# Cross-attention, feed-forward and quantised layers in one kernel: values with keys on the partitions, weights converted into the token buffers, first loads in order of use, fewer warm-up products

## What is computed

```python
query = layernorm(x) @ w_q.T        # 2 x 512 tokens, 1024 features
key   = ctx_4096 @ w_k.T            # 2 x 1024 context rows, 256 features
value = ctx_4096 @ w_v.T            # 2 x 1024 context rows, 256 features
...
att = softmax(query_h @ key_g.T / sqrt(32), masked) @ value_g
x = x + att @ w_out.T
```

## Time and profile before

| | us |
|---|---|
| median of 3 runs | 1073.83 (1072.63 to 1076.23) |
| the profiled execution | 1075.11 |
| its span in the trace | 1073.3 |
| PE busy | 1032.0 |
| DVE busy | 874.6 |
| stage a, start to the last product of PE | 200.5 |

### The profile page before, as it was taken

The page is one execution under the profiler, slowest core; times in us unless marked ns, Lnnn a source line. Parts: engine busy times, 40 slices in busy tenths (PEclk is TensorE's granted clock), DMA queues, the critical chain, the costliest instruction groups (busy, mean ns, idle before and its releaser), DMA issues. The chain is left out here.

```text
span 1073.3 us, 20195 instructions
## 1 busy us (share of the span) xinstructions
PE 1032.0 (96%) x7174; PEld 780.3 (73%) x7174; DVE 874.6 (81%) x1881; ACT 663.5 (62%) x1127; POOL 93.8 (9%) x85
## 2 busy tenths in 40 slices
PE   8999999999999999999999999999999999956978
PEld 7888888777777777777777777776888887534637
DVE  5764544799999999999999999975764895879998
ACT  5332320498989899898998989862331114635826
POOL 0221011200000000000000000000002112400000
PEclk9999999999999999999999999999999999987989
DMA  8548779841123232123323212158315000000003
GB/s 328 182 166 297 258 262 280 314 121 37 45 75 73 68 73 70 37 45 73 73 68 73 66 39 48 50 202 276 118 59 171 0 0 1 1 1 1 1 1 156
DMA packets 55568, 112.95 MB, mean 105 GB/s; under 512 B 7724, under 2 KB 21164, under 8 KB 55388
## 3 DMA queue, kind: packets, MB, share of 16 engines
q1 hardware_dynamic: 55452, 112.26, 33.6%
q0 software_dynamic: 64, 0.00, 0.0%
HBM read 83.99 MB, written 27.26 MB: 104 GB/s over the span
## 5 line engine op out<-in xcount | busy, mean ns | idle before, releaser
L898 DVE CUSTOM_DVE_ANT_0 XS<-b_psS,b_mbias 128x1024 f32<-128x1024 f32 x256 | 311.1, 1215 | 0.9 <-PE b_psS L778 0.7
L853 ACT ACTIVATE XS<-XS,b_mins 128x1024 f32<-128x1024 f32 x256 | 295.5, 1154 | 10.1 <-DVE b_mins L898 9.5
L811 PEld LDWEIGHTS b_psT<-ident,XS 128*128 128x128 f32 x2048 | 229.9, 140 | 65.8 <-issue 47.6
L811 PE MATMUL b_psT<-ident,XS 128*128 128x128 f32 x2048 | 271.9, 276 | 1.6 <-ACT b_PT L861 1.6
L907 DVE COPY b_PT<-b_psT 128x512 f32<-128x512 f32 x256 | 176.9, 691 | 26.8 <-PE b_psT L811 25.1
L861 ACT COPY b_PT<-b_psT 128x512 f32<-128x512 f32 x256 | 149.7, 585 | 38.8 <-PE b_psT L811 30.8
L778 PE MATMUL b_psS<-XTh 128*128 128x512 f32 x512 | 155.9, 422 | 0.7 <-PEq L115 0.6
L792 PE MATMUL b_psO<-b_PT,XTh 128*32 128x256 f32 x1984 | 132.8, 385 | 0.0
L778 PEld LDWEIGHTS b_psS<-XTh 128*128 128x128 f32 x512 | 85.1, 189 | 18.5 <-DVE b_mins L898 7.7
L792 PEld LDWEIGHTS b_psO<-b_PT,XTh 128*32 128x32 f32 x1984 | 51.8, 109 | 42.1 <-issue 20.8
L415 ACT ACTIVATE a_oh<-a_psM 128x512 fp32r<-128x512 f32 x24 | 14.2, 597 | 80.1 <-PE a_psM L335 53.5
(11 more groups left out here) (270 smaller groups left out, 1613.9 us busy)
## 6 DMA issues: line engine op xcount, KB each, us to landing
XS<-in_ctx SPq DMA_DIRECT2D x16, 512.0 KB, 5.6
XTh<-QHd SPq DMA_DIRECT2D x32, 256.0 KB, 4.5
XTh<-QLd SPq DMA_DIRECT2D x32, 256.0 KB, 5.0
XS<-in_ctx_turned SPq DMA_DIRECT2D x8, 512.0 KB, 10.9
XS<-in_x SPq DMA_DIRECT2D x8, 512.0 KB, 11.9
a_wst<-in_L_xattn_w_q SPq DMA_DIRECT2D x8, 512.0 KB, 5.5
a_xn<-in_ctx_turned SPq DMA_DIRECT2D x8, 512.0 KB, 4.1
QHd<-a_oh SPq DMA_DIRECT2D x16, 256.0 KB, 5.4
```

Source lines behind the costliest of these rows:

```text
L811: last_t = pe.transpose(psT[:, kt, :], Pr[:, k % PR, kt * P:(kt + 1) * P], ident[:])
L853: act.activation(Pr[:, k % PR, :], Sc[:, k % 4, :], ACT.Exp, bias=mins[:, k % 4:k % 4 + 1], scale=-1.0, accum_out=sums[:, u, j:j + 1]).the ...
L898: dve.tensor_tensor_reduce(out=Sc[:, k % 4, :], in0=psS[:, k % 2, :], in1=mbias[:, qt, :], scale=1.0, scalar=3.4e38, op0=ALU.add, op1=ALU.min,
```

## The change

Values are computed with keys on the partitions: a context tile of 128 keys is now the stationary operand, and the 256 features of both value weight tiles are the moving columns. One product `m` covers two key tiles, 2 x 8 x 3 = 48 matmuls of 256 columns. `turn_v`, `vT` and `keep_product` are gone; `keep_values` copies straight from `psM` to `vst`, of which batch 0 has its own, `XS[:, 0:2, :]`. Both weight tiles must be split before the first of these products. They are converted into buffers of the tokens: batch 0's into the columns of the last two token tiles of `XTh`/`XTl`, batch 1's into `XTl` alone, after the last query product. Batch 1's order becomes K tile 0, V, K tile 1. At the start the loads are cut and ordered by use, and the first context tile is split in halves. `keep_warm` runs 13 products. POOL's two scalar transfers are issued after its third normalised tile, and it waits for batch 0's values to be stored before it scales `q2`. In stage b ACT waits for the store of batch 1's values ahead of its second exponential.

```diff
+        vst = [XS[:, r:r + 2, :].rearrange(...) for r in (0, 5)]
-        vT = (q2[:].rearrange("p a n -> p (a n)").bitcast(F32), XS[:, 4, :])
...
+        def hi_lo(w):
+            if V0 <= w < Q0:
+                c = slice(TOK - (Q0 - w) * P, TOK - (Q0 - w - 1) * P)
+                return XTh[:, :, c], XTl[:, :, c]
+            if V1 <= w < K1_LAST:
+                return tuple(XTl[:, i * KVT + w - V1, :].rearrange("p (k n) -> p k n", k=KT) for i in range(2))
+            return WTh[:, w % 2, :, :], WTl[:, w % 2, :, :]
...
@@ SP
-            load_ctx0(0)
-            load_w(0)
-            load_w(1)
-            for k in range(1, KT):
+            load_first_w(0, PART[0])
+            load_ctx0(0)
+            load_first_w(1, PART[0])
+            for k in range(1, 3):
+                load_ctx0(k)
+            for w in range(2):
+                load_first_w(w, PART[1])
+            for k in range(3, KT):
                 load_ctx0(k)
...
             for k in range(2):
                 load_ctx1(k)
+            store_values(0)
             for t in range(KT):
...
@@ PE
+            def values(m):
+                pe.wait_ge(w_split, tile_parts(Q0 - 1 if m < M_Q else K1_LAST - 1))
+                pe.wait_ge(mm_free, m + 1)
+                for half in range(2):
+                    kt = first_key_tile(m) + half
+                    out = psM[:, m % 4, half * KVT * P:(half + 1) * KVT * P].rearrange("p (w n) -> p w n", w=KVT)
+                    for k in range(KT):
+                        vh, vl = value_weights(m, k)
+                        for i, (a, b) in enumerate(((CTh, vh), (CTh, vl), (CTl, vh))):
+                            last = pe.matmul(out, a[:, k, kt * P:(kt + 1) * P], b, start=(k == 0 and i == 0),
+                                             stop=(k == KT - 1 and i == 2))
...
-            keep_warm(pe, psM[:, 3, 0:P], ident, 20)
+            keep_warm(pe, psM[:, 3, 0:P], ident, 13)
...
-                if m < M_Q + KVT:
-                    turn_v(m - M_Q)
...
@@ ACT
+                if w >= V1:
+                    act.wait_ge(mm_done, M_K1)
...
+            weights_hi(2)
+            weights_hi(3)
             act.wait_ge(setup, 3)
             root(0)
...
@@ DVE
+            def keep_values(m):
+                first = first_key_tile(m)
                 dve.wait_ge(mm_done, m + 1)
+                if m == M_V0:
+                    dve.wait_ge(xn_ready, 2)
+                dve.tensor_copy(vst[int(m >= M_V1)][:, :, first:first + 2, :].rearrange("p g k d -> p k g d"),
+                                psM[:, m % 4, :].rearrange("p (k g d) -> p k g d", k=2, g=GROUPS)).then_inc(mm_free, 1)
...
@@ POOL
-            pool.dma_start(qs[:, 0:1], quant[2].partition_broadcast(P)).then_inc(par, 16)
-            pool.dma_start(qs[:, 1:2], quant[3].partition_broadcast(P)).then_inc(par, 16)
             for t in range(NT):
+                if t == 3:
+                    pool.dma_start(qs[:, 0:1], quant[2].partition_broadcast(P)).then_inc(par, 16)
+                    pool.dma_start(qs[:, 1:2], quant[3].partition_broadcast(P)).then_inc(par, 16)
...
             pool.wait_ge(par_ready, 1)
+            pool.wait_ge(v_stored, 16)
...
@@ stage b, ACT
+                if first and k == 1:
+                    act.wait_ge(hand.v_stored, 16 * B)
```

More of the change, by code:

```diff
@@ L127, in stage_a @@
         cst = XS[:, 2:4, :]
[L128 removed]
+        vst = [XS[:, r:r + 2, :].rearrange("p a n -> p (a n)").rearrange("p (g k d) -> p g k d", g=GROUPS, k=NK)
+               for r in (0, 5)]
         qy = XS[:, 0:2, :]
@@ L151, in stage_a @@
         w_in = [sem(f"a_w{u}") for u in range(2)]
+        w_first = [sem(f"a_wf{u}") for u in range(2)]
         q_in = [sem(f"a_q{u}") for u in range(2)]
@@ L361, in _ @@
             pe.wait_ge(setup, 2)
-            keep_warm(pe, psM[:, 3, 0:P], ident, 20)
+            keep_warm(pe, psM[:, 3, 0:P], ident, 13)
             first_keys()
             pe.wait_ge(setup, 3)
-            for i in range(4):
-                product(2 * V0 + i, CTh, CTl)
+            for i in range(2 * KVT):
+                values(M_V0 + i)
                 turn_x(2 * i)
@@ L369, in _ @@
             pe.wait_ge(x_split, NT // 2)
-            for m in range(M_Q, M_V1):
+            for m in range(M_Q, M_K1):
                 if m == M_Q + 1:
@@ L373, in _ @@
                 product(m, XTh, XTl)
-                if m < M_Q + KVT:
-                    turn_v(m - M_Q)
-            pe.wait_ge(c_split, 2 * KT)
-            for m in range(M_V1, 2 * NW):
-                product(m, CTh, CTl)
-                if m == M_V1 + 2:
-                    turn_v(2)
-                elif m == M_K1:
-                    turn_v(3)
+            pe.wait_ge(c_split, 2 * KT + 1)
+            for m in range(M_K1, 2 * NW):
+                if is_value(m):
+                    values(m)
+                else:
+                    product(m, CTh, CTl)
             pe.wait_ge(mm_free, 2 * NW - 4 + 1 + 4)
@@ L524, in quantise @@
                                   ).then_inc(q_step, 1)
-            ctx_lo(0)
-            weights_lo(0)
-            weights_lo(1)
-            for k in range(1, KT):
-                ctx_lo(k)
+            first_weights_lo(0, 0)
+            first_ctx_lo(0)
+            first_ctx_lo(1)
+            first_weights_lo(1, 0)
+            for k in range(1, 3):
+                ctx_lo(k)
+            for w in range(2):
+                first_weights_lo(w, 1)
+            for k in range(3, KT):
+                ctx_lo(k)
+            weights_lo(2)
+            weights_lo(3)
             moments(0)
```

253 lines of the change are left out of this document (130 added, 123 removed).

## The result

The changed kernel takes 1068.29 us (median of four executions, 1068.1 to 1068.61) where the kernel before takes 1074.17 (1072.63 to 1076.23). The ratio is 0.9948, with a 95% interval of 0.9936 to 0.9961: 0.5% faster. The forecast was 1066.8 us, with a range of 1062.5 to 1073.0. The profiled execution took 1068.61 us with a span of 1066.8, against 1075.11 and 1073.3.

A forecast was written before the change was run, and what follows sets the result against it. PE's own work was taken to bound stage a, after one early 3.4 us wait. The terms -6.7 - 3.5 + 2.9 + 0.3 = -7.0 us took the median from 1073.83 to 1066.8 us, range 1062.5 to 1073.0.

The forecast's parts named there:

- What bounds stage a: Stage a: after the 3.4 us wait for weight tile 1 all is PE's own work, moving the end one for one.
- The trough: Loads, 6 to 8 us: DMA at 78 GB/s, taken to go once POOL's two scalar transfers are moved.
- Rival (1): Start: the trough stays, context tile 1 lands at 10.9 us; -1.7 us, 1072.1 us; chance 0.33 with part of a trough.
- The start, -6.7: Start of stage a: context tile 1 split by 9.3 us, no PE wait after it, first products end at 28.4; -6.7 us.
- The turns, -3.5: Value stage: four of eight transposes with the restart behind them, 0.88 us each, go; -3.5 us.
- The value products, +2.9: Value stage: 384 products of 256 columns at 0.121 us, 46.5 us, replace 192 of 512, 43.6 us; +2.9 us.
- Rival (2): Value products: weight load not hidden, 0.188 us each; +18.7 us in all, 1092.5 us; chance 0.09 with other new PE waits.
- Rival (3): Value products: 256 columns cost only 0.112 us each, -0.6 instead of +2.9 us; 1063.3 us; chance 0.10.
- rival (4): Start: fewer warm-ups leave PE at 1.2 GHz for twelve products, 5.1 us; 1068.9 us; chance 0.48 together with the forecast.
- Hidden work: Stage a: moved splits, POOL's wait for stored values and late weight tile 14 make PE wait for nothing; counted as none.
- The start of stage b, +0.3: Start of stage b: ACT's second exponential waits for batch 1's values' store, between 0 and 0.9 us; +0.3 us taken.
- the chances: Whole kernel: below 1070.6 us 0.66, within 0.3% of no change 0.25, slower 0.09.

The follow-up runs named there:

- the first two experiments: POOL's two scalar transfers back at the start of the changed kernel, 1073.05 us; the same transfers put behind the third token tile in the kernel before, 1070.7 us.
- the second profile: The changed kernel measured and profiled once more without any edit, on one chip with two further versions: 1068.59 us, ratio 0.9952.

## Why the prediction was right, and where it was off

**What bounds stage a.** Right. From context tile 1 on PE never waits in stage a, and each edit of the start or of the values moved the end of stage a one for one.

**The trough.** I had only a coincidence in time for it, and the first two experiments show that it was the cause: without POOL's two transfers at the start there is none, with them there is, in either kernel. Rival (1), the trough stays, falls; the rule of the Trainium skill, DMA: Bandwidth & Descriptors, section Issuing engines are not separate DMA queues, weighed ahead, that all transfers share 16 engines and interleave, does not keep tiny pieces from costing 3 to 5 us here. What the forecast did not see is that these pieces hold up a stream from SP's queue as from POOL's, and that their place decides.

**The start, -6.7 for -5.67: a term mis-sized.** Two steps of it failed. Context tile 1 was to land at 7.0 and be split at 9.3; ACT got it at 8.15 (8.30 in the second profile), and PE at 10.53. I had let the stream run at 414 GB/s from the first tile on, but it moved 232 in 2 to 4 us and 334 in 4 to 6, and 333 and 256 in the second profile. And PE was to be free at 6.3, worked out from the mean of 40 warm-up rows (0.175 us), when the first of them take 0.21 and only the later 0.11; the 26 ended at 7.14. That cost nothing beside the first, since PE still paused for context tile 1. And the 5.67 flatter the change: they start from the long execution of the kernel before, and by the medians the start gave nearer 4.4 (3.2 for the scalars in the kernel before, 1.15 for the rest). Most of its gain is the place of the scalars (3.2 to 4.8 us), where I had thought of the order of loads as its equal partner (it gives, with halves and warm-ups, 1.15, a third to a half of it by the warm-ups).

**The turns, -3.5 for about -3.3.** Right; the -3.3 are what the products leave of the whole, not a reading of their own.

**The value products, +2.9 for +2.0.** The model (a fixed part and the rest by columns) gave 0.121 us, measured were 0.1187. The bound of 0.112 is what a product of 128 columns takes. Rival (2), 0.188, falls: rows of weight loads overlap one another, so their length is no price. Rival (3), 0.112 for 256 columns, falls too, by 2.6 us in all. The estimate of 41.9 us by the Trainium skill, TensorE: Matmul & The Clock Gate, section Back-to-back issue gap, is 3.7 too low here; the section gives that rule for a single product, and other figures for a stream of products with loads.

**The clock, rival (4).** With 13 warm-up calls the twelve first products ran at the full rate, so it did not come about; without them it did: the twelve took from 7.04 to 12.30, 5.3 us where the rival said 5.1, and the first value product came 1.93 us later.

**Hidden work.** Right: nothing of DVE's, POOL's or SP's moved work made PE wait. **The start of stage b, +0.3 for +0.07:** the values' store was issued at 191.30 and landed in 4.8 us, before 197, while ACT's second exponential starts at 199.07.

**The sum.** -7.0 for -6.5 in the profiles is nearer than its terms: the start was taken 1.0 us too high and the values 0.9 too dear, and the two errors nearly cancel. That is luck. One figure in the chances is also added up wrongly: the parts named for a time below 1070.6 make 0.69, not 0.66.

**From the profile to the median.** The forecast for the profiled execution was 1068.1, and 1068.61 came. For the median it was 1066.8, and 1068.29 came; 1.0 us of these 1.5 is the step that took the profiled execution to stand 1.3 us above the median after as before. It stands 0.3 above after. The executions of the kernel before reach over 3.6 us (1072.63 to 1076.23), those of the changed one over 0.5, and over 1.35 in its second set. The same divide runs through the experiments: with POOL's scalars at the start 3.4 and 2.3 us, without 0.4 to 1.5. I read this as a trough that falls a little differently each time, and did not test it.

**Left open:** why 4-byte pieces hold up the stream, what the 0.112 us of a product of 128 columns consist of, why the old order with halved weights starts so late, and why the trough sets in before POOL's packets are seen.

## What to carry to other kernels

Look for transfers made of tiny pieces ahead of, or beside, the loads that the first products need, and move them to where a tile has slack; here that was worth three to four times as much as ordering and halving the loads and the fewer warm-ups together. An fp32r product with its own weight load could be made narrower down to 256 columns here (0.1187 us, about half of the 0.227 for 512); below that it cost the same for less work (0.112 for 128). When a start is shortened, find the one tile that the chain hangs on; starting earlier than it lands gave 0.1 us here. And where executions of a kernel scatter over 3 us, do not read a gain of 1 us from one profile of it.

## What the runs showed of the hardware

- A broadcast of one 4-byte scalar to 128 partitions took 6.8 and 7.4 us to land when SP issued two of them into the first loads, and the stream fell from 383 to 60 GB/s for 2 us. From POOL's queue they took 7.0 to 8.6 us, and the stream fell to 78 GB/s (the kernel before) and 189 (the changed one) in 6 to 8 us. Issued at 37.8 us, at the end of the loads, they took 3.1 and 4.0 us.
- A load is there only when the last of its 16 shares has landed, and the others run ahead. In the changed kernel's trace the 16 landing signals of context tile 1 lie between 7.06 and 8.13 us; its last byte is 1.57 MB into the stream, and 2.03 MB had been moved at its end (249 GB/s on the mean over 8.15 us). In the kernel before, with the trough, those of weight tile 1 lie between 6.35 and 10.91 us.
- Weight loads of fp32r whose rows are 188 to 192 ns long follow each other every 112 ns. bf16 products of 128 columns with their own load stand 56 ns apart, fp32r and f32 ones 112.
- In the program's first microseconds products ran at half the rate (0.427 us for 512 columns, 0.21 for a warm-up) while the clock in the record was 1.00. Later, after a pause, half rate and a record of 0.50 go together.
